# A three-layer mixture-of-experts and scan kernel: five linked empty GpSimd instructions before 231 of 512 indirect transfers, two shared scatter targets, a new head, a sigmoid gate and a new order of stages

## The reference

```python
x = x + 0.5 * ffn(layernorm(x))       # layer f = 0
x = x + attn(layernorm(x))
x = x + 0.5 * ffn(layernorm(x))       # layer f = 1

def ffn(x):        # 16 experts, 2 per token, hidden size 256
    logits = x @ Wr + br;  w, idx = top_k(softmax(logits), 2);  w /= sum(w)
    return x + sum over the two of w * (gelu(x @ W1[e] + b1[e]) @ W2[e] + b2[e])

def attn(x):       # a gated linear recurrence with a complex factor
    q, k, v, a, g = xn @ (wq, wk, wv, wa, wg)
    a = sigmoid(|a|) * exp(1j * angle(a))
    y_t = a_t * y_(t-1) + k_t * v_t          # along the 256 tokens
    return (q * real(y) * silu(g)) @ wo
```

## Time and profile before

| | |
|---|---|
| median of 3 runs | 994.97 us (992.37 to 1000.95) |
| span of the profiled execution | 994.3 us |
| TensorE, weight loads, VectorE, ScalarE, GpSimd busy | 725.1, 607.2, 546.3, 514.7, 590.6 us |
| DMA | 167.13 MB, 168 GB/s on average |

### The profile page before, as it was taken

How to read it: one execution, slowest core, us unless ns; L and a number is a source line. 1 busy time by engine, 2 the same in 40 slices (tenths; PEclk the granted TensorE clock), 3 DMA queues, 4 the chain that set the end, 5 groups by cost and what they waited for, 6 DMA issues and landing times.

```text
span 994.3 us, 15862 instructions
## 1 busy us (share of the span) xinstructions
PE 725.1 (73%) x4409; PEld 607.2 (61%) x4410; DVE 546.3 (55%) x1352; ACT 514.7 (52%) x1071; POOL 590.6 (59%) x551
## 2 busy tenths in 40 slices
PE   4775888786876888669777967685968648977761
PEld 4234788685366873469644867534958627777650
DVE  7983103106689955799745996647876455010201
ACT  1111556455777637676277773576664315444340
POOL 2277441555777747758467457378657545655555
PEclk9995899889977989789788779795989759999986
DMA  9995587774146833176441456321758517778863
GB/s 327 299 348 165 149 234 228 208 202 130 40 123 195 224 111 105 42 202 194 121 124 46 129 161 202 99 66 40 217 167 250 141 41 199 221 207 226 234 201 103
DMA packets 188846, 167.13 MB, mean 168 GB/s; under 512 B 18976, under 2 KB 176480, under 8 KB 187744
## 3 DMA queue, kind: packets, MB, share of 16 engines
q1 hardware_dynamic: 120736, 106.83, 36.6%
q0 software_dynamic: 16384, 33.72, 11.5%
q10 hardware_dynamic: 51648, 25.63, 8.8%
HBM read 104.57 MB, written 61.51 MB: 167 GB/s over the span
## 4 chain that ended last, share of the span: by engine, by line
PE 48%; issue 12%; ACT 12%; another core or an unknown queue 9%; SPq 7%; DVE 5%; DMA 5%; ACTq 0%; DVEq 0%
PE bank L786 17%; PE bank L803 16%; PE bank L863 7%; DMA WUP<-up_weights 4%; PE bank L776 4%; ACT eo L540 2%; SPq L319 2%; PE bank L758 2%; SPq L360 1%; SPq L330 1%; ACT hidT L532 1%; PE bank L702 1%; ACT ci L623 1%; ACT xsT L551 1%
## 5 line engine op out<-in xcount | busy, mean ns | idle before, releaser
L487 POOL DMA_INDIRECT got<-rows_out,IDX x256 | 285.8, 1117 | 194.2 <-ACT eo L540 86.5
L786 PE MATMUL bank<-xsT,WUP 128*128 128x128 f32 x1564 | 240.0, 303 | 77.4 <-ACT xsT L551 51.1
L786 PEld LDWEIGHTS bank<-xsT,WUP 128*128 128x128 f32 x1564 | 218.8, 216 | 85.9 <-issue 75.2
L803 PE MATMUL bank<-W,hidT 128*128 x1564 | 221.0, 286 | 41.5 <-ACT hidT L532 32.1
L803 PEld LDWEIGHTS bank<-W,hidT 128*128 128x128 f32 x1564 | 199.3, 199 | 51.4 <-issue 49.6
L466 POOL DMA_INDIRECT rows_in<-XL,IDX x128 | 157.1, 1227 | 109.3 <-DVE IDX L1039 46.5
L474 POOL DMA_INDIRECT rows_in<-XL,IDX x128 | 136.3, 1065 | 91.7 <-ACT eo L540 53.7
L540 ACT ACTIVATE eo<-bank,xs 128x128 f32<-128x128 f32 x391 | 122.7, 367 | 109.9 <-PE bank L803 74.6
L532 ACT ACTIVATE hidT<-bank 128x512 f32<-128x512 f32 x200 | 118.1, 591 | 116.1 <-PE bank L786 72.8
L551 ACT ACTIVATE xsT<-bank 128x256 f32<-128x256 f32 x200 | 74.0, 377 | 86.2 <-remote 39.2
L863 PE MATMUL bank<-XT,WA 128*128 128x512 f32 x192 | 94.6, 654 | 21.2 <-DVE qg L1090 10.4
(11 more groups left out here) (150 smaller groups left out, 900.4 us busy)
## 6 DMA issues: line engine op xcount, KB each, us to landing
WUP<-up_weights SPq DMA_DIRECT2D x400, 128.0 KB
xs<-rows_in SPq DMA_DIRECT2D x100, 258.0 KB
rows_out<-eo ACTq DMA_DIRECT2D x91, 256.0 KB
rows_in<-kv SPq DMA_DIRECT2D x16, 774.0 KB, 12.1
X<-in_L_attn_x SPq DMA_DIRECT2D x4, 1024.0 KB, 7.7
rows_in<-XL,IDX POOLq DMA_INDIRECT x256
got<-rows_out,IDX POOLq DMA_INDIRECT x256
out<-X SPq DMA_DIRECT2D x4, 1024.0 KB
```

The lines of the kernel that those rows point to most:

```text
L487: pool.indirect_dma_start(got[:, k, j, :], None, rows_out[SLOT[f, g, half]][0:rows, :], bass.IndirectOffsetOnAxis(IDX[:, g, j, k:k + 1], 0 ...
L786: ins = pe.matmul(ps[2 + u % 2][:, k * P:(k + 1) * P], WUP[:, u, a, c * P:(c + 1) * P], xsT[:, u % 2, a * P:(a + 1) * P], start=True, stop ...
L803: ins = pe.matmul(o, hidT[:, v, (2 * a + c) * P:(2 * a + c + 1) * P], W2[:, ds(e * H + c * D, D)], start=(c == 0), stop=(c == 1))
```

## The change

- **Empty instructions.** A table APART marks 231 of the 512 indirect transfers; ahead of each GpSimd issues five `engine_nop`, each linked (it raises the chain's semaphore and GpSimd waits for it). By stage: P(0,0) 22 of 32, P(0,1) 26, G(0,0) 19, P(0,2) 13, G(0,1) 11, P(0,3) 15, G(0,2) 6, P(1,0) 19, G(0,3) 8, P(1,1) 14, G(1,0) 15, P(1,2) 11, G(1,1) 17, P(1,3) 13, G(1,2) 19, G(1,3) 3.
- **Pacing.** PAIRS_BY and PRODUCTS_BY hold small numbers: pair counts end at 64 instead of 199, product counts at 45 instead of 92.
- **Scatter targets.** Two rows_in arrays are used in turn (g % 2), and a part of rows_out[0] for the second half of layer (1,3), which has a rows_out of its own. Two arrays are cleared instead of four. A scatter waits until the layer that used its target before has done all of its pairs.
- **Layout.** A tile now holds 128 consecutive tokens (x_v, out_v are "(g b) (l p) d -> g p (b l) d"): loads and stores of X have runs of 512 B, XT's copies and `project` read and write contiguous columns, and the angle's constants differ by halves of 32 columns.
- **Head.** X of group 0 comes in quarters, measured as they arrive; for f = 0 ScalarE normalizes half of XL (a new stage M); X of group 1 is issued behind the up weights.
- **Gate.** A sigmoid of the gap gives the second weight and one minus it the first (a stage Q of its own on ScalarE); Exp, an addition and a reciprocal go. `invert` (H) first loads a table that has Ln and Exp.
- **XN** lies in cr instead of kv, so the attention's normalization may come ahead of A3.
- **VectorE.** The correction of X (L980) moves from R to W; pairs of operations are merged into one of both; a few small ones go.
- **Order.** ORDER is new. Between K and the next T an expert layer is no longer cut around A3: before E(0,2) had parts 0-8, 8-20, A3, 20-24; now 0-8, 8-24, A3. Layer (0,1) is cut at 12, (0,3) at 8 and 16, (1,0) at 4, (1,1) at 8, (1,2) at 4 and 8; the biases of (1,3) are the last TensorE work.

```diff
+APART = {
+         ("P", 0, 0, 0): (0, 0, 0, 1, 1, 1, 1, 1, 1, 1, 1, 1, 1, 1, 0, 1, 1, 1, 1, 1, 1, 1, 1, 0, 0, 0, 0, 0, 0, 1, 1, 1),
...
+ROWS = {(f, g, h): 2 if h else g % 2 for f, g, h in SLOT}
+OUT = {(f, g, h): G if h else g for f, g, h in SLOT}
...
-    x_v = x.rearrange("(g b) (c l) d -> g (b c) l d", g=G, l=T)
+    x_v = x.rearrange("(g b) (l p) d -> g p (b l) d", g=G, p=P)
...
-        XN = kv[:].rearrange("p (l d) -> p l d", l=T)
+        XN = cr[:].rearrange("p (l d) -> p l d", l=T)
...
-            sp.dma_start(X[:, 0, :, :], x_v[0]).then_inc(x_in[0], 16)
+            for i in range(4):
+                quarter = slice(i * T // 4, (i + 1) * T // 4)
+                sp.dma_start(X[:, 0, quarter, :], x_v[0][:, quarter, :]).then_inc(first_in[i], 16)
...
-            clear(2)
-            clear(3)
...
+            def keep_apart(st, i):
+                if APART[st][i]:
+                    link(pool.engine_nop())
+                    link(pool.engine_nop())
+                    link(pool.engine_nop())
+                    link(pool.engine_nop())
+                    link(pool.engine_nop())
...
-                pool.wait_ge(zeroed[slot], 16 * ZEROS)
+                if half:
+                    pool.wait_ge(combined, 4 * (gathers.index((1, 0)) + 1))
+                elif f == 0 and g < 2:
+                    pool.wait_ge(zeroed[into], 16 * ZEROS)
+                else:
+                    pool.wait_ge(eo_sb, pairs_by[(f, g - 2, 0) if g > 1 else (0, g + 2, 0)])
...
+            def normalize_rows(normed, n, f, g):
+                act.wait_ge(norm_ready, normed)
...
+                for j in range(T // 2, T):
+                    ins = act.activation(XL[:, n % XBUF, j, 0:D], X[:, g, j, :], ACT.Identity,
+                                         scale=rs[:, j:j + 1], bias=nb[:, j:j + 1])
...
-                act.activation(gexp[:], gap[:], ACT.Exp).then_inc(gap_exp, 1)
+                act.activation(share[:], gap[:], ACT.Sigmoid).then_inc(share_ready, 1)
...
-                    act.activation(by_time(XT[:])[:, 4 * i:4 * i + 4, :], ps[i][:].rearrange("p (l c) -> p l c", l=4), ACT.Copy,
-                                   scale=GS[:, 0:1]).then_inc(xnT_sb, 1)
+                    act.activation(XT[:, i * 512:(i + 1) * 512], ps[i][:], ACT.Copy, scale=GS[:, 0:1]).then_inc(xnT_sb, 1)
...
             def invert(n):
+                act.preload_act_table_set("natural_log_exp_and_others")
...
-                        ins = pe.matmul(ps[4 + i][:, j * D:(j + 1) * D], by_time(kv[:])[:, 4 * i + j, :], WO[:],
+                        ins = pe.matmul(ps[4 + i][:, j * D:(j + 1) * D], kv[:, (4 * i + j) * P:(4 * i + j + 1) * P], WO[:],
...
-                xl, xg = XL[:, n % XBUF, :, 0:D], X[:, g, :, :]
-                dve.wait_ge(xl_ready, (T // 4) * (n + 1))
-                dve.scalar_tensor_tensor(out=xg, in0=xl, scalar=LIFT, in1=xg, op0=sub, op1=add)
...
-                    link(dve.tensor_scalar(den[:], gexp[:], 1.0, None, add))
-                    link(dve.reciprocal(den[:], den[:]))
+                    dve.tensor_scalar(WGT[:, g, 0, :], share[:], -0.5, 0.5, mult, add)
+                    dve.tensor_scalar(WGT[:, g, 1, :], share[:], 0.5, None, mult)
```

More of the change, by code:

```diff
@@ L31 @@
 ZEROS = 4
+SHARED = (0,)
 EPS = 1e-5
@@ L176, in rows_put, with rows_normed @@
                                        and kind_no[st] <= rn and kind_no[st] % XBUF == rn % XBUF)
+    def rows_normed(n):
+        by_act = 2 * sum(st[1] in SHARED for st in kind_no if st[0] == "R" and kind_no[st] < n)
+        return 4 * n - by_act, by_act
     with ExitStack() as ctx:
@@ L505, in normalize @@
                         ins.then_inc(xn_ready_act, 1)
+            def normalize_rows(normed, n, f, g):
+                act.wait_ge(norm_ready, normed)
+                for st in kind_no:
+                    if st[0] == "K" and kind_no[("R",) + st[1:3]] == n - XBUF:
+                        which, count = rows_put(*st[1:])
+                        act.wait_ge(scattered[which], count)
+                for j in range(T // 2, T):
+                    ins = act.activation(XL[:, n % XBUF, j, 0:D], X[:, g, j, :], ACT.Identity,
+                                         scale=rs[:, j:j + 1], bias=nb[:, j:j + 1])
+                    if j % 4 == 3:
+                        ins.then_inc(xl_ready_act, 1)
             def route(n):
@@ L991, in route @@
                 dve.tensor_tensor(gap[:], MX[:, :, 1], MX[:, :, 0], sub).then_inc(gap_ready, 1)
-                for k in range(2):
-                    ins = dve.tensor_tensor(hot[:, k, :, :], LG, MX[:, :, k:k + 1].broadcast_to([P, T, E]), ALU.is_equal)
-                link(ins)
+                best = MX[:, :, 0:2].rearrange("p t k -> p k t").unsqueeze(3).broadcast_to([P, 2, T, E])
+                link(dve.tensor_tensor(hot, LG.unsqueeze(1).broadcast_to([P, 2, T, E]), best, ALU.is_equal))
                 for k in range(2):
@@ L1050, in rank, with weigh @@
                                          op0=mult, op1=add).then_inc(experts_ready, 1)
-            def weigh(g):
-                for k in range(2):
-                    ins = dve.tensor_tensor(hot[:, k, :, :], hot[:, k, :, :],
-                                            WGT[:, g, k, :].unsqueeze(2).broadcast_to([P, T, E]), mult)
-                link(ins)
+            def weigh(n, g):
+                xl, xg = XL[:, n % XBUF, :, 0:D], X[:, g, :, :]
+                by_dve, by_act = rows_normed(n + 1)
+                dve.wait_ge(xl_ready, by_dve)
+                dve.wait_ge(xl_ready_act, by_act)
+                dve.scalar_tensor_tensor(out=xg, in0=xl, scalar=LIFT, in1=xg, op0=sub, op1=add)
+                link(dve.tensor_tensor(hot, hot, WGT[:, g, :, :].unsqueeze(3).broadcast_to([P, 2, T, E]), mult))
                 dve.tensor_tensor(LG[:], hot[:, 0, :, :], hot[:, 1, :, :], add).then_inc(comb_ready, 1)
@@ L1102, in phase @@
                 dve.wait_ge(proj_ps, 24 * (n + 1))
-                link(dve.tensor_scalar(XT[:], tmp[3], -2.0, PI / 2, mult, add))
+                for w, corner in enumerate((PI / 2, -PI / 2)):
+                    steps16 = [part.rearrange("p (n w t) -> p n w t", w=2, t=16)[:, :, w, :] for part in (XT[:], tmp[3])]
+                    ins = dve.tensor_scalar(steps16[0], steps16[1], -2.0, corner, mult, add)
+                link(ins)
                 link(dve.scalar_tensor_tensor(out=XT[:], in0=cr[:], scalar=0.0, in1=XT[:], op0=ALU.is_lt, op1=mult))
-                fourth = XT[:].rearrange("p (t f) -> p t f", f=4)[:, :, 3:4]
-                link(dve.tensor_scalar(fourth, fourth, -PI, None, add))
                 run = C * T
```

103 lines of the change are left out of this document (56 added, 47 removed), and 160 rows, old and new, of tables (APART, ORDER, PAIRS_BY, PRODUCTS_BY).

## The result

The changed kernel takes 1089.5 us (median of 4 runs, 1080.8 to 1095.7), the kernel before 994.1 beside it: ratio 1.092, 95% interval 1.085 to 1.100. It is slower by 9.2%. The forecast was 943 us and faster, and the range ended at 986. Ratios and their intervals use only a kernel's fast runs, those within 1.5% of its fastest, while medians are of all its runs, so the two can differ by about a percent.

What follows compares the result with a forecast made beforehand. TensorE was taken as the bound through hand-ordered stages ending in waits, with no engine full. The parts summed to -46 us, 5 more came off: 994.3 - 51 = 943 us; own range 930 to 958 (55%), with rivals 918 to 986 (8 in 10).

Steps and rivals of the forecast that it cites:

- GpSimd after the head: Transfers after the first ones: 231 sets cost 115 us, nearly all pacing waits go, mostly hidden; +5 us (0 to +40).
- price of a set: Five linked empty instructions ahead of a transfer on GpSimd: at least 0.3 us, at most 1.8, taken as 0.5.
- transfers crowd the weights: Rival, 12% to 15% in kind: expert pairs beside unpaced transfers slow by up to 0.24 us on 200 pairs, +48, so 991; chance 15%.
- a rival of its own (926 us): Stalls without a name shrink or miss the path; one of 16.9 us goes, giving 926 us; chance 11%.
- Switches: From a group's output projection to the next attention: 18.7 us instead of 27.3 to 33.2; 35 us saved with the wait ahead.
- Output projection: Attention's output projection on TensorE: contiguous weights make it 4.3 us instead of 7.26; the fourth one saves 3.0 us.
- VectorE, head: X's correction leaves the router's chain, -4.6 us; at the start, earlier indices against 22 sets of empty instructions, +2 us.
- Tables: ScalarE's table loads: one instead of two ahead of the reciprocal saves 10 us, the gate's sigmoid 4.5 us.
- Pairs beside transfers: Expert pairs on TensorE: 2.2 us each without indirect transfers, 3.0 us with them.
- Sum of the local savings: Whole kernel: the parts sum to -46 us, and 5 us more are taken off, giving 943 us.
- GpSimd the bound: Rival: five empty instructions at 1.0 us make GpSimd's chain set the time, 1036 us; chance 7%.
- Slow single transfers, and the stall without a name: A transfer took 3.15 us instead of 0.97 beside VectorE; VectorE stood still 16.89 us ahead of the last router's logits.

Runs made afterwards that it cites:

- r4: The kernel before with all its pacing counts set to 0, so transfers wait only for their data: 1225.7 us, ratio 1.216.
- r18_before_sets_on_all: The kernel before with five linked empty instructions ahead of each of its 512 transfers, nothing else changed: 959.5 us, ratio 0.980.
- second group: Four runs of variants of the changed kernel on one chip, where the kernel before took 885.2 us; their ratios were 1.007, 1.001, 1.067 and 0.967.
- r8_unlinked: The changed kernel with its 231 sets of five empty instructions not linked, where the kernel before took 885.2 us: 856.4 us, ratio 0.967.
- r1_no_empty: The changed kernel with all 231 marks of APART set to 0, so no empty instructions: 1223.7 us, ratio 1.226 to the kernel before.
- r14_sets_on_all: The changed kernel with five linked empty instructions ahead of all 512 transfers instead of 231: 955.2 us, ratio 0.971 to the kernel before.

## Why the prediction was wrong

**The step that failed** is the one on GpSimd after the head: "Nearly all pacing waits go [...] so it is mostly hidden", +5 us (0 to +40). It counted the waits only as time that GpSimd gets back. They broke up the runs of dense transfers, and without them completions on other engines come late: +215 to +229 us in the kernel before (r4), +220 in the changed one (1223.7 against 1004.1), where no sets stand in between. The sets then give 134 of these back. The price of a set was over-estimated: 0.57 - 0.30 = 0.27 us instead of 0.5 (and less than the 0.3 called its least), so 62 us instead of 115; beside the lag this hardly matters.

**The rival "transfers crowd the weights"** had the place and the direction right, at 15%. What was mis-sized is its term: "0.24 us on 200 pairs: +48" scaled the 0.8 us of contention by the ratio of the rates, as if a pair slowed in proportion. With transfers 1.25 to 1.38 us apart pairs don't slow by 0.24 us, they stop, for up to 10.8 us at a time in the changed kernel, wherever the kernel before takes 979 to 997 us. "Against it: their number is fixed, so a burst buys quiet later" was wrong for the same reason: the loss isn't linear in the rate, so a burst costs more than quiet gives. The rates were wrong as well: 1.43 us, called the unpaced distance, is the mean; 297 distances of the kernel before were already under 1.3.

**The warning stood in the rows.** The earlier trace rows give 9% of the chain to an unknown queue, 89 us, and the VectorE wait of 16.89 us is of the same kind: an engine waits for TensorE's products. TensorE's last product for it and one of the gathers, in the timeline of before:

```profile
792.11 1.89 PE L712 MATMUL bank<-WR,hidT 128*128 128x16 f32 x8 [0.24 <-issue]
799.44 0.94 POOL L487 DMA_INDIRECT got<-rows_out,IDX  x1 [0.30 <-issue]
800.69 0.95 POOL L487 DMA_INDIRECT got<-rows_out,IDX  x1 [0.30 <-issue]
```

The product ends at 794.00 and VectorE starts at 801.48, 7.5 us later; fourteen gathers, 1.25 us apart from the second on, start between 783 and 801. In r18_before_sets_on_all, where they are 1.51 us apart:

```profile
770.58 1.87 PE L727 MATMUL bank<-WR,hidT 128*128 128x16 f32 x8
772.55 0.42 DVE L1000 TENSOR_TENSOR ranks<-bank,BR 128x256 f32<-128x256 f32 x1 [19.11 <-issue]
```

There VectorE starts 0.1 us behind the product. So 7.5 of the 16.89 us were the lag, and the rest is VectorE with nothing to do. The prediction read it as one odd stall and gave it a rival of its own (926 us). On the chip of the second group the unknown share is absent, and the kernel before takes 110 us less. That these two numbers are near each other fits, but no trace of the kernel before was taken on that chip. The range failed with it: a releaser without a name was no ground for a gain only, it was a cost that the change could multiply.

**Point by point.**
- *Switches*, -35: right in the trace. 27.3 and 33.2 us became 10.5, 9.4 and 7.1. The middle one before was counted as 30.3 and is 32.4 in the trace (475.88 to 508.31), so 65.9 us go; less the four pairs and the bias that moved (11.1 us each), 32.6 remain.
- *Output projection*, 4.3 us: 3.84 to 4.02 in three of four, 6.34 in one.
- *VectorE, head*, +2: the first scatter starts at 38.74 instead of some 42, and the first expert layer at 95.3 instead of 93.6.
- *Tables*, -14.5: half. Ahead of the reciprocal there is one load of 1.28 us instead of two, but it still runs after the gates' last copy (324.10, behind 323.48), so the wait of TensorE in the router is 3.1 us instead of 4.16, not 1.7. In all six loads go, 7.7 us.
- *Pairs beside transfers*: 132 records in 16 us, 2.2 us per pair, beside 13 transfers in r8_unlinked, as fast as the 2.2 that I had without any. So what looked like contention at 3.0 us a pair may in part have been the same lag; no run separates the two on one chip.
- *Sum of the local savings*: with the lag absent and next to no sets, the ratio is 0.967, where the forecast was 943/994 = 0.948 and its range ended at 0.991. They are real, at 29 of 51 us; the rest I can't place, as this run and the kernel before differ in the waits too.
- *GpSimd the bound*: no. In the changed kernel GpSimd idles 23.85 us ahead of the last gathers, for the results of the last expert pairs. With 512 sets it is the bound.

**Slow single transfers, and the stall without a name.** The prediction had one transfer of 3.15 us beside VectorE. The traces have many: in the kernel before, 69 transfers run mostly beside a TENSOR_TENSOR or SCALAR_TENSOR_TENSOR of VectorE that is over 1.5 us long, and 52 of them take over 1.5 us (the medians are 2.0 us). The 210 beside no VectorE instruction take 1.00 us at most. The changed kernel shows the same (51 of 69; the longest is 3.68 us, at 49.57). The Trainium skill (SBUF — State Buffer, "Who interferes with whom") infers that a tensor_tensor leaves descriptor writing alone; these rows disagree. Such transfers are as frequent in r8_unlinked, on the chip without the lag (57 of 76). The Trainium skill (Runtime: NRT & Kernel Launch, "Instruction fetch mechanics") was set against the 16.89 us. The amount of code was not the cause, and here the trace agrees: r18_before_sets_on_all has 2560 instructions more than the kernel before, in the same order, and its lateness at this place is 0.1 us.

**What stays open.** Which part of the chip is late (the matmuls themselves, or the news of them), and what of a transfer crowds it: its issue, its packets or its completion; no run varied them apart. Why chips differ, and whether it is the chip or what ran beside the kernel at that hour: the fast kind was met once, in one group, the other in five groups on four chips. Also the changed kernel's own time on the fast kind. There its relatives stand at 0.967 (unlinked), 1.001 and 1.007 (one old table more), so it may well be no slower than before; this is argued, not shown.

## What to carry to other kernels

A wait that seems to cost only an idle engine may be what keeps a shared resource from overload: before it is removed, take it away alone in the old kernel and time that. Where many indirect transfers go out, plot the time against the distance between two of them; here the step from 1.38 to 1.51 us was worth 122 us, and a plain filler instruction does most of it. Waits that break up a row of dense transfers do nearly as much: they brought 1.23 to 1.01, the five linked ones on all 512 to 0.97. And a gain of a few per cent is a statement about one chip until it is measured on another; here the same kernel stood at 0.97 and 1.18.

## What the runs showed of the hardware that I had not expected

- Beside indirect transfers 1.25 us apart, where the kernel before takes 979 to 997 us, engines start on TensorE's finished groups late: 6.5, 10.4 and 7.5 us in the three cases above (by the modelled ends), with single waits up to 10.8 us, and 21 us on the same two lines in r1_no_empty. Four weight issues of SyncE took 5.81 instead of 2.11 us, with the DMA engines at 31% and TensorE's granted clock at 0.50. With all of them at least 1.51 us apart no such wait is over 3.4 us (r14_sets_on_all, r18_before_sets_on_all).
- The step is steep: 1.10, 1.00, 0.97 at 1.38, 1.44 and 1.51 us, each on a chip of its own.
- Chips differ by 11% on one and the same kernel (885 and 979 to 997 us). A part probably sits in this lag: 157 us of unnamed waits in the one trace of the slower kind, none in four traces of its relatives on the faster. With all transfers 1.51 us apart the same kernel takes 947 and 955, but there GpSimd is the bound on both, which would hide a difference elsewhere.
- A linked empty instruction widens the distance from one transfer to the next by 0.054 us, an unlinked one by 0.01.
- An indirect transfer's issue takes some 2 us instead of 0.95 beside a VectorE TENSOR_TENSOR or SCALAR_TENSOR_TENSOR of 2048 columns in SBUF (medians of 69 transfers in the kernel before and 76 in r8_unlinked), on either kind of chip.
